# Shared experts with both pairs of banks, statistics tile by tile, and a closing addition on GpSimd, in a four-layer decoder on one NeuronCore

## What is computed

```python
def _layernorm(x, axis=-1, eps=1e-05):
    m = jnp.mean(x, axis=axis, keepdims=True)
    v = jnp.var(x, axis=axis, keepdims=True)
    return (x - m) / jnp.sqrt(v + eps)
...
    scores = jax.nn.sigmoid(logits)
    _, idx = jax.lax.top_k(scores + bias[None, :], K)
    w = jnp.take_along_axis(scores, idx, axis=-1)
    w = w / jnp.clip(jnp.sum(w, axis=-1, keepdims=True), 1e-12, None)
...
    out = yrows.reshape(-1, K, D).sum(axis=1)
    out = out + jax.nn.silu(X @ sw1.T) * (X @ sw3.T) @ sw2.T
```

## Time and profile before

| what | value |
|---|---|
| median of three runs (2465.91 to 2471.26) | 2468.8 us |
| the profiled execution: its own time | 2461.88 us |
| the profiled execution: its span | 2460.1 us |
| TensorE busy, share of the span | 2149.3 us, 87% |
| VectorE | 1741.0 us, 71% |
| ScalarE | 1215.2 us, 48% |
| GpSimd | 1171.4 us, 48% |
| mean granted TensorE clock | 0.920 |

### The profile page before, as it was taken

One profiled execution on the slowest core, in us unless ns is written; L12 is line 12 of the kernel. 1 busy time (PEld: TensorE's weight loads), 2 busy tenths in 40 slices (PEclk: granted clock), 3 DMA queues, 4 the chain that ended last, 5 costly groups with the idle time before them and its releaser, 6 DMA issues. The chain is left out here.

```text
span 2460.1 us, 37815 instructions
## 1 busy us (share of the span) xinstructions
PE 2149.3 (87%) x12822; PEld 1486.7 (60%) x12822; DVE 1741.0 (71%) x3657; ACT 1215.2 (49%) x2508; POOL 1171.4 (48%) x1350
## 2 busy tenths in 40 slices
PE   6998779677899986658999999999999976879788
PEld 3666557455688854455666666666666635557555
DVE  5778668655788865765776877777766664479398
ACT  6888545323566652234444444444444433444355
POOL 5331028001699940117766776677666600014198
PEclk8999879868999997768999999999999988989899
DMA  1000016000766610012443434333433341000184
GB/s 48 2 3 2 7 34 135 7 6 21 163 158 150 156 24 20 0 68 39 91 99 80 101 76 100 77 103 92 88 79 86 70 76 40 1 0 1 35 184 107
DMA packets 64904, 161.92 MB, mean 66 GB/s; under 512 B 7995, under 2 KB 19003, under 8 KB 57416
## 3 DMA queue, kind: packets, MB, share of 16 engines
q1 hardware_dynamic: 64712, 159.50, 28.1%
HBM read 156.46 MB, written 3.01 MB: 65 GB/s over the span
## 5 line engine op out<-in xcount | busy, mean ns | idle before, releaser
L2325 PE MATMUL bank<-l2h_og,l2h_wo 128*128 128x512 f32 x512 | 260.4, 593 | 2.0 <-DVE LNT L2586 1.6
L2435 ACT ACTIVATE l2h_pr<-twin,l2h_nmx 128x512 f32<-128x512 f32 x256 | 176.1, 688 | 151.9 <-PE bank L2314 105.0
L2427 ACT ACTIVATE l2h_prT<-bank 128x512 f32<-128x512 f32 x256 | 151.8, 593 | 195.1 <-PE bank L2314 195.1
L1149 POOL TENSOR_TENSOR l1m_hid_lo<-l1m_hid,l1m_hid_hi 128x512 fp32r<-128x512 f32 x128 | 210.4, 1663 | 47.8 <-ACT l1m_hid_hi L1082 47.5
L2589 DVE TENSOR_REDUCE l2h_nmx<-twin 128x2 f32<-128x1024 f32 x128 | 156.2, 1220 | 93.1 <-PE twin L2303 93.0
L2664 POOL TENSOR_TENSOR l2h_vs<-l2h_vg 128x256 f32<-128x256 f32 x256 | 193.2, 754 | 20.2 <-DVE l2h_vg L2562 20.2
L2562 DVE TENSOR_TENSOR l2h_vg<-bank,l2h_gv 128x512 f32<-128x512 f32 x256 | 175.0, 684 | 34.5 <-POOL l2h_vs L2664 21.8
L2574 DVE TENSOR_TENSOR l2h_og<-bank,l2h_gt 128x512 f32<-128x512 f32 x256 | 173.3, 680 | 4.9 <-PE bank L2325 2.7
L2053 POOL TENSOR_TENSOR l3x_pr<-l3x_pr,l3x_rs 128x1232 f32<-128x1232 f32 x16 | 36.0, 2250 | 273.5 <-DVE l3x_rs L2074 273.5
L2659 POOL TENSOR_TENSOR l2h_plain<-l2h_plain,l2h_rotated 128x512 f32<-128x512 f32 x64 | 82.6, 1291 | 172.5 <-DVE l2h_rotated L2555 172.5
L2314 PE MATMUL bank<-ident,l2h_pr 128*128 128x128 f32 x1024 | 160.8, 280 | 0.0
(11 more groups left out here) (606 smaller groups left out, 5946.4 us busy)
## 6 DMA issues: line engine op xcount, KB each, us to landing
l2h_gt<-l2m_gate_rows SPq DMA_DIRECT2D x128, 512.0 KB, 7.2
l1m_c<-l1m_weights SPq DMA_DIRECT2D x62, 512.0 KB, 6.4
l3m_c<-l3m_weights SPq DMA_DIRECT2D x30, 512.0 KB, 6.5
l0m_c<-l0m_weights SPq DMA_DIRECT2D x14, 512.0 KB, 6.7
l1m_w<-in_l1m_pairs SPq DMA_DIRECT2D x32, 192.0 KB, 6.5
l2h_fresh<-in_l2m_wqkv SPq DMA_DIRECT2D x8, 768.0 KB, 4.3
l2h_wo<-in_l2m_wo SPq DMA_DIRECT2D x8, 512.0 KB, 3.8
l0m_w<-in_l0m_pairs SPq DMA_DIRECT2D x8, 192.0 KB, 5.2
```

The source lines that it names most:

```text
L1149: nc.gpsimd.tensor_tensor(hid_lo[:, h % RING, :], hid[:, h % 4, :], hid_hi[:, h % RING, :], ALU.subtract)\
L2325: nc.tensor.matmul(ybank[:, :], wo[s][:, e, :], og[:, e % 4, :], start=(e == 0), stop=(e == E - 1))\
L2427: nc.scalar.activation(prT[:, j // 2 % 2, h, :, j % 2 * P:(j % 2 + 1) * P], tbank[:, :].rearrange("p (c q) -> p c q", c=TPB), ACT.Copy).th ...
L2435: nc.scalar.activation(pr[:, h, :], sbank[:, h, :], ACT.Exp, bias=nmx[:, k % 2, h:h + 1], accum_out=rs[:, g % 2, t, h:h + 1]).then_inc(exp ...
```

## The change

1. A class `Trailing` takes statistics of single tiles. In both kinds of context attention, `token_stats` after every fourth tile gives way to: after the addition of tile t, `bn_aggr` of tile t-2 and `bn_stats` of tile t-1; the rest after the loop.
2. In l3m `AHEAD` becomes 2 and the count bank is bank 4. The counting matmuls move ahead of the last `shared_down`. The products move: one after the replacing of the maxima, one after the mask, one inside `normalized` ahead of the multiplication by the reciprocal, one after it.
3. In l0m one product goes into the loop over the two group maxima instead of ahead of it (fill tuple (1, 1, ...) to (0, 1, ...), with `fill(1)` called twice).
4. In l1m the product between the maxima of the groups and their replacement moves to inside `normalized`.
5. The closing addition of layer 2 moves from VectorE to GpSimd, with a semaphore `summed`; VectorE only takes the statistics.

```diff
+class Trailing:
...
+    def counted(self, ins, t):
+        self.T.dve_steps += 1
+        ins.then_inc(self.T.dve_step, 1)
+        self.step[t] = self.T.dve_steps
+
+    def stats(self, t):
+        self.counted(self.nc.vector.bn_stats(self.T.ln_stats[:, t, :], self.src[:, t, :]), t)
+
+    def aggregate(self, t):
+        self.dve.wait_ge(self.T.dve_step, self.step[t])
+        self.nc.vector.bn_aggr(self.T.ln_mv[:, t, :], self.T.ln_stats[:, t, :])
+        self.T.ln_known.append(t)
...
                         nc.vector.tensor_tensor(xt, xt, obank[tile % 2][:, 0:D], ALU.add).then_inc(added, 1)
-                        if tile % TPB == TPB - 1:
-                            dve.wait_ge(added, tile + 1)
-                            token_stats(nc, T, link, T.X[:, :, :], batch_tiles(tile // TPB))
+                        if tile >= 2:
+                            trailing.aggregate(tile - 2)
+                        if tile >= 1:
+                            dve.wait_ge(added, tile)
+                            trailing.stats(tile - 1)
                     read(pieces_at(i))
+                trailing.aggregate(NT - 2)
+                dve.wait_ge(added, NT)
+                trailing.stats(NT - 1)
+                trailing.aggregate(NT - 1)
...
-            T.chosen, T.counts, T.count_bank = st.sem("chosen"), st.sem("counts"), T.bank[5]
+            T.chosen, T.counts, T.count_bank = st.sem("chosen"), st.sem("counts"), T.bank[4]
...
-        AHEAD = 1 if counted else 2
+        AHEAD = 2
...
-                shared_down(PRE - 1)
                 if counted:
...
                     last.then_inc(T.counts, 1)
+                shared_down(PRE - 1)
                 pe.wait_ge(routed, 1)
...
         for _ in range(TG):
             pick_max(nc, link, gs, T.rev[:, 64 - NG:64], gm, c, O)
-        fill(1)
+            fill(1)
...
-def normalized(nc, rt, link, cw, scale, floor, clip):
+def normalized(nc, rt, link, cw, scale, floor, clip, between=None):
...
+    if between is not None:
+        between()
     link(nc.vector.tensor_tensor(cw[:, :, :], cw[:, :, :], spread(total, E), ALU.mult))
...
-        fill = fill_parts(shared_product, (1, 1, 0, 0, 1, 1))
+        fill = fill_parts(shared_product, (0, 1, 0, 0, 1, 1))
...
-        fill = fill_parts(shared_product, (2, 1, 1, 1, 1, 1))
+        fill = fill_parts(shared_product, (2, 0, 1, 1, 1, 1))
...
-        normalized(nc, rt, link, cw, 1.0, 1e-20, False)
+        normalized(nc, rt, link, cw, 1.0, 1e-20, False, shared_product)
...
-        fill = fill_parts(shared_product, (1, 1))
+        fill = fill_parts(shared_product, (0, 1))
...
         chosen_scores(nc, link, V, score, cw)
+        normalized(nc, rt, link, cw, 1.0, 1e-12, True, shared_product)
         shared_product()
-        normalized(nc, rt, link, cw, 1.0, 1e-12, True)
...
                 for b in range(B):
+                    dve.wait_ge(T.summed, b + 1)
+                    token_stats(nc, T, link, T.X[:, :, :], batch_tiles(b))
+
+            @block.gpsimd
+            def _(pool):
+                for b in range(B):
                     ts = slice(b * TPB, (b + 1) * TPB)
-                    link(nc.vector.tensor_tensor(T.X[:, ts, :], T.X[:, ts, :], T.LNX[:, ts, :], ALU.add))
-                    token_stats(nc, T, link, T.X[:, :, :], batch_tiles(b))
+                    nc.gpsimd.tensor_tensor(T.X[:, ts, :], T.X[:, ts, :], T.LNX[:, ts, :], ALU.add).then_inc(T.summed, 1)
```

More of the change, by code:

```diff
@@ L67, in token_stats, with __init__ @@
     return out
+class Trailing:
+    def __init__(self, nc, T, dve, src):
+        self.nc, self.T, self.dve, self.src = nc, T, dve, src
+        self.step = {}
+    def counted(self, ins, t):
[8 more added lines that the diff above has]
+        self.T.ln_known.append(t)
 def batch_tiles(b):
@@ L763, in move @@
                     return nc.vector.tensor_scalar(to, frm, scale, bias, ALU.mult, ALU.add)
+                trailing = Trailing(nc, T, dve, T.X[:, :, :])
                 def rotate(b, n):
@@ L2079, in _ @@
                         nc.vector.tensor_tensor(x, x, obank[j % 2][:, 0:D], ALU.add).then_inc(added, 1)
-                        if j % TPB == TPB - 1:
-                            dve.wait_ge(added, j + 1)
-                            token_stats(nc, T, link, T.X[:, :, :], batch_tiles(j // TPB))
+                        if j >= 2:
+                            trailing.aggregate(j - 2)
+                        if j >= 1:
+                            dve.wait_ge(added, j)
+                            trailing.stats(j - 1)
+                trailing.aggregate(NT - 2)
+                dve.wait_ge(added, NT)
+                trailing.stats(NT - 1)
+                trailing.aggregate(NT - 1)
 def l3_attentions(nc, T, A):
@@ L2784, in build @@
         T.bank = single[0:2] + [T.twin[:, 0, :], T.twin[:, 1, :]] + single[2:6]
-        T.dve_step, T.ln_var, T.ln_std, T.ln_scaled, T.ln_even, T.ln_odd, T.ln_affine, T.ln_turned, inputs, stored = (
+        T.summed, T.dve_step, T.ln_var, T.ln_std, T.ln_scaled, T.ln_even, T.ln_odd, T.ln_affine, T.ln_turned, inputs, stored = (
             ctx.enter_context(nc.semaphore(n))
-            for n in ("dve_step", "ln_var", "ln_std", "ln_scaled", "ln_even", "ln_odd", "ln_affine", "ln_turned", "inputs", "stored"))
+            for n in ("summed", "dve_step", "ln_var", "ln_std", "ln_scaled", "ln_even", "ln_odd", "ln_affine", "ln_turned", "inputs", "stored"))
         with nc.Block() as block:
```

## The result

The changed kernel takes **2440.22 us** (median of four runs, 2431.68 to 2446.44) where the kernel before takes 2467.36 (four runs); the ratio is 0.989, 95% interval 0.9865 to 0.9915. That is 27.1 us faster. I had forecast 2455.5 and a range down to 2449: the direction was right, the size half of what came.

What follows compares the result with a forecast made beforehand. The prediction took the kernel as a chain of stages, with TensorE waiting for VectorE at the seats changed. Gains of 5.0 + 2.3 + 1.4 + 0.25 + 1.4 + 1.6 + 1.3 = 13.3 us gave 2455.5, range 2449 to 2465.

Steps and rivals of the forecast that it cites:

- the sum: Over the seven changed places: gains add to 13.3 us off the profiled execution's 2461.9, giving 2448.6.
- Statistics by tile: In the context attentions of layers 0, 2 and 3: single-tile statistics save 1.4, 1.6 and 0.25 us.
- Closing block: At layer 2's end: additions on GpSimd while VectorE takes statistics, 6.5 us for 7.7, 1.3 saved.
- rival (b): In layer 2's closing block GpSimd and VectorE take turns: 2.6 us less gain, total 2458; chance 8%.
- Routing: In the expert stages of layers 3, 0 and 1: shorter waits save 5.0, 2.3 and 1.4 us.
- (c): In layer 3's expert routing the second pair of banks does little: gain 2.5 us there, total 2458; chance 15%.
- (e): In the routings, moving the products changes nothing, the path being TensorE's: 8.7 us less gain, 2464; chance 3%.
- Rival (a): In the three context-attention loops each tile's statistics cost 0.55 instead of 0.28 us: 6.5 less gain, 2462; chance 7%.
- Rival (d): In the experts' loops TensorE's clock falls back to half, making the kernel slower: 2474 us; chance 3%.
- The step from the profiled run to the median: For the whole kernel: the profiled execution, 6.9 us below the median of 2468.8, keeps that difference, giving 2455.5.

## Why the prediction was wrong, point by point

**The step that failed** is the one under the sum, that "a stage shortened by 1 us shortens the whole by about that, if the work after it is the same", together with the prices taken for TensorE's work that the change does not touch. The work after it was the same, its clock was not. Two terms were mis-sized by it: the statistics, 14.5 us for 3.3, and the closing block, 6.4 for 1.3.

- **Statistics by tile**, forecast 3.3, measured 14.5. In place the prices were near: the steps of l3x that had been 5.1 and 6.4 are 5.4, with one of 5.75, and l0x shortened by 2.0 for 1.4. What I left out is that the placement of the statistics also moves TensorE's clock. In l2x I took the tail as fixed at 1.7 us a tile; those 1.7 were matmuls at half clock, and became 0.90 in the runs with statistics by tile and the old routing. That is 8 us in one stage for a forecast of 1.6. In the changed kernel the clock falls in that tail all the same, and the stage gained 4.2 in one profile and 1.8 in the other. After l0x the clock rises some 12 us sooner in the next stage, which is 2.5 us shorter up to the end of its router and 4.8 in the whole. Of the 14.5, the single loops account for 7.3; the rest is open.
- **Closing block**, forecast 1.3, measured 6.4. In its place 1.5, so the sum was right there, and so was the reading of the port: rival (b) is out. The other 5 are the clock behind the block: padded back to 18.5 us, they are gone. In the profiles of these two runs l3a, where the clock rises 5 us sooner or later, takes 107.6 and 113.5. In the changed kernel run again the block is as short and the rise is late, so these 5 us are not sure in every run.
- **Routing**, forecast 8.7, measured 10.9 in total, and 5.3, 2.0 and 2.3 in place for 5.0, 2.3 and 1.4. Rivals (c) and (e) are out. What comes late now is the counting, as said. In l1m I had TensorE lose 1.1 us on a late product; it waits 0.61 for the last one, less than before, and the last gate holds VectorE up by 0.14 (610.41 + 0.25 to 610.80). That is why l1m gave 2.3.
- **Rival (a)** is out: the steps of l3x are 5.4, with one of 5.75, not all over 5.6, and no stage of the three became longer.
- **Rival (d)** had the right account and the wrong sign. I looked at the clock as something to lose in the experts' loops; it was gained in the short stages with gaps, and the mean over the run went from 0.918 (the median of twelve runs of the kernel before) to 0.925 (of six runs of the changed one).
- **The step from the profiled run to the median** ("I take the same difference off the median") cost as much as the sum's own errors: 15.4 between the profiles, 27.1 between the medians. The profiled run of before was one of those with the short l3a, 107.6, and no row of a single trace can tell that this is not the usual case. That the difference of the two profiles, 15.4, came near the 13.3 of the sum is luck.
- **The range**: its lower end is the upper bounds of all terms and 3 us for the spread of the runs, and all these bounds were worked out at the clock of one trace. A clock of another pattern was in none of them, though its worth, 36 us at half clock for 18 of time, stood in rival (d).

## What to carry to other kernels

Where short bursts of TensorE stand between waits, read the granted clock of each stage beside its time, before pricing anything: an edit that only removes a stop of 1 to 2 us can be worth several times that in the matmuls behind it, and in the next stage. Take more than one profile of the same kernel, and compare stages that nobody touched; if they differ by more than the gain looked for, the sum from one trace needs a range as wide as that. Test a gain by the clock with an edit that moves nothing else, as the extra matmul and the padded block do here. Cheap matmuls where TensorE would stand idle at a hand-over are worth a trial.

## What was not expected of the hardware

- The same program's l3a takes 107.6 or 113.6 us, and its l2a 56.3 or 60.5, by the clock alone: l3a was at half clock for 22 or 41 us, l2a for 5 or 15.
- Adding 2.2 us to a block cost nothing measurable (ratio 0.9998, 0.9982 to 1.0014), and adding 1.3 to a shorter one took its gain from 0.9973 back to 1.0008. In the profiles l3a's time falls into groups: five at 107.5 to 108.3, three at 110.1 to 112.7, seven at 113.5 to 113.7, three at 116.2 to 116.3.
- GpSimd's addition of 128x512 takes 1.23 us from start to start beside `bn_stats` of VectorE, and does not lengthen it: 0.87 for four with and without. The Trainium skill's SBUF — State Buffer, section SBUF: two separate sides, names VectorE instructions with two SBUF inputs, or in a two-port mode, for the lock that VectorE and GpSimd share; `bn_stats` has one input, and these rows agree.
